# A conv, attention and expert kernel on one core: GpSimd's second addition of a round placed behind the first of the next

## The reference

```
x = x + conv3x3(groupnorm(x, 32 groups), sign(weight))
t = tokens(x)                                  # 3136 tokens of 64 channels per image
n = layernorm(t)
q, k, v = n Wq, n Wk, n Wv                     # one head of 32
t = t + softmax(q k^T / sqrt(32)) v Wo + b_o + n
n = layernorm(t)
w = softmax(mean over images of n, Wr)         # 8 gates per token
t = t + sum over 8 experts of w_e * (relu(bn(relu(bn(n W1_e)) W2_e)) Wo_e + bo_e)
```

## Time and profile before

| | |
|---|---|
| median of 3 runs | 7050.26 us (7049.38 to 7055.04) |
| the profiled execution | 7055.03 us, of which the span of instructions is 7053.2 |
| granted TensorE clock, mean | 0.986 |
| PE, POOL, DVE, ACT busy | 6827.4, 5472.6, 5077.8, 4355.5 us |
| a steady slot | 180.0 us |
| last attention slot (image 31) | about 5740 to 5902 us |
| start of the second block | about 5933 us |

### The profile page before, as it was taken

How to read it: one execution, slowest core, us unless ns; L and a number is a source line. 1 busy time by engine, 2 the same in 40 slices (tenths; PEclk the granted TensorE clock), 3 DMA queues, 4 the chain that set the end, 5 groups by cost and what they waited for, 6 DMA issues and landing times. The chain is left out here.

```text
span 7053.2 us, 132108 instructions
## 1 busy us (share of the span) xinstructions
PE 6827.4 (97%) x50610; PEld 3615.0 (51%) x50610; DVE 5077.8 (72%) x9184; ACT 4355.5 (62%) x9296; POOL 5472.6 (78%) x5522
## 2 busy tenths in 40 slices
PE   6999999999999999999999999999999997999999
PEld 3555555555555555555555555555555553333333
DVE  6777777777777777777777777777777762655565
ACT  1666666666666666666666666666666664555555
POOL 2888888888888888888888888888888895222222
PEclk7999999999999999999999999999999997999999
DMA  1111111111111111111111111111111002444443
GB/s 31 15 24 24 24 24 24 24 24 24 24 24 24 24 24 24 24 24 24 20 19 24 24 24 24 24 24 24 24 24 24 10 10 56 100 101 103 101 102 93
DMA packets 328980, 248.83 MB, mean 35 GB/s; under 512 B 253672, under 2 KB 311408, under 8 KB 324256
## 3 DMA queue, kind: packets, MB, share of 16 engines
q1 hardware_dynamic: 316064, 214.68, 13.7%
q0 software_dynamic: 12288, 25.71, 1.8%
HBM read 162.70 MB, written 77.59 MB: 34 GB/s over the span
## 5 line engine op out<-in xcount | busy, mean ns | idle before, releaser
L618 ACT ACTIVATE probs<-bank 128x392 f32<-128x392 f32 x6400 | 2796.9, 496 | 1887.0 <-PE bank L667 1841.0
L481 DVE TENSOR_REDUCE part_max<-bank 128x1 f32<-128x448 f32 x5600 | 3213.3, 614 | 583.9 <-PE bank L660 573.8
L660 PE MATMUL bank<-ks,qs 96*128 96x448 f32 x5600 | 2347.9, 424 | 55.3 <-DVE part_max L481 50.0
L428 POOL TENSOR_TENSOR psum<-psum,probs 128x392 f32<-128x392 f32 x2048 | 2098.6, 1025 | 318.3 <-ACT probs L618 33.1
L425 POOL TENSOR_TENSOR psum<-probs 128x392 f32<-128x392 f32 x2048 | 2099.5, 1025 | 240.9 <-ACT probs L618 229.5
L667 PE MATMUL bank<-qs,ks 97*128 97x392 f32 x6400 | 2027.4, 367 | 15.6 <-ACT probs L618 13.3
L676 PE MATMUL bank<-probs,vs 128*32 128x392 f32 x12288 | 1768.2, 507 | 34.1 <-POOL psum L428 26.6
L678 PE MATMUL bank<-psum,ones 128*32 128x392 f32 x4096 | 1740.7, 507 | 0.0
L660 PEld LDWEIGHTS bank<-ks,qs 96*128 96x128 f32 x5600 | 1065.5, 190 | 1230.8 <-DVE part_max L481 745.5
L667 PEld LDWEIGHTS bank<-qs,ks 97*128 97x128 f32 x6400 | 1191.7, 190 | 407.0 <-ACT probs L618 223.0
L985 ACT ACTIVATE h<-l_bank,xin 128x392 f32<-128x392 f32 x1024 | 639.0, 674 | 445.1 <-PE l_bank L1079 445.1
(11 more groups left out here) (126 smaller groups left out, 5740.3 us busy)
## 6 DMA issues: line engine op xcount, KB each, us to landing
xin<-in_x_dram SPq DMA_DIRECT2D x64, 784.0 KB, 8.9
xs<-x_dram SPq DMA_DIRECT2D x512, 98.0 KB, 2.5
xpk<-in_x_dram SPq DMA_DIRECT2D x64, 392.0 KB, 12.6
t_dram<-t SPq DMA_DIRECT2D x32, 784.0 KB, 5.3
x_dram<-xn SPq DMA_DIRECT2D x32, 784.0 KB, 6.9
res<-t_dram SPq DMA_DIRECT2D x256, 98.0 KB, 2.7
out_dram<-fin POOLq DMA_DIRECT2D x256, 98.0 KB, 2.8
gate_w<-gate_dram SPq DMA_DIRECT2D x16, 392.0 KB, 5.2
```

The source lines that it names most:

```text
L428: add = gp.tensor_tensor(into, into, three, ALU.add)
L481: v.tensor_reduce(part_max[:, b, m:m + 1], m_bank[place.bank()][:, 0:MW], AX.X, ALU.max).then_inc(m_used, 1)
L618: s.activation(probs[:, held(c, k), :], s_bank[n % 3][:, 0:2 * QW], ACT.Exp, scale=SCALE).then_inc(p_ready, 1)
L660: mm(m_bank[place.bank()][:, 0:MW], qs[par][0:KS, b * P:(b + 1) * P], ks[par][0:KS, m * MW:(m + 1) * MW], start=True, stop=True).then_inc( ...
```

## The change

In a round, the second add leaves the step `sum` and becomes a step of its own, `third`, whose place is 3.1 units (`GROUP + 0.1`) behind `sum`: just behind the `sum` of the next round, which is 3 units on. The add of the half block becomes the step `tail`, 2.8 units behind the last `third` of a chunk. Steps that fall past the slot's end go to `norms`. `sum_part` now counts first adds alone; a new semaphore `round_part` tells `tail` of the last `third`. What is added, and in which order within a round, is the same.

Beside it the places of other steps are changed: `sum` 0.29 units earlier, `apply` 1.2 later, `gather` 0.3 earlier; `stats` with 2.72 units between them instead of 2.18; `moments`, `pair` and `shift` (which hang on `PAD_AT`) 5.69 later, the four `pad` steps at 123.5, 140.4, 157.3 and 174.2 instead of 117.8, 135.5, 153.2 and 170.9; `conv` 1, `var` 1 and `var` 3 of `prepare` (with what hangs on them) by 0.4 to 0.7; `fetch` 0.37 and `store` 7.17 earlier. In the order that results, `moments` comes between the first and second reciprocal of the divide of c = 3 (before: ahead of `max` of block 7, 6), and `pair` between scores 20 and 21 of c = 4 on PE (before: between 14 and 15, ahead of `project` of c = 3).

```diff
--- before.py
+++ after.py
@@ -69,16 +69,16 @@
 DVE_LAG = 0
 VALUE_AFTER = HELD - VISIT
 VISIT_AT, DOOR = 0.0, 1
-SUM_LAG, APPLY_LAG = 1.22, 3.72
-GATHER_AFTER, DIVIDE_AFTER, DIVIDE_STEP = -0.19, 0.1, 0.73
-STATS_AT, STATS_STEP, PAD_AT, PAD_STEP = 93.6, 2.18, 117.81, 17.71
-PREPARE_AT = (0.4, 2.6, 5.3, 7.6, 19.2, 19.9, 25.4, 28.1, 30.6, 32.6, 35.9, 38.6)
+SUM_LAG, APPLY_LAG = 0.93, 4.92
+GATHER_AFTER, DIVIDE_AFTER, DIVIDE_STEP = -0.49, 0.1, 0.73
+STATS_AT, STATS_STEP, PAD_AT, PAD_STEP = 93.6, 2.72, 123.5, 16.9
+PREPARE_AT = (0.4, 2.6, 6.0, 7.6, 19.2, 19.9, 24.9, 28.1, 30.6, 32.6, 35.9, 39.0)
 NORMS_AT = (69.7, 74.5, 77.8, 81.9, 92.7, 95.9, 101.3, 106.5)
 PROJ_AT, PROJ_STEP = 12.23, 3.3
 VALUES_AT = (50.8, 58.0)
 BORDER, LAST_MAX = 58.0, 9.34
 ROW_AFTER = (1.2, 4.1)
-FETCH_AT, STORE_AT = 60.89, 113.0
+FETCH_AT, STORE_AT = 60.52, 105.83
 
 
 def visit_at(n):
@@ -116,7 +116,11 @@
         order += [(c * BLOCKS + k + 0.5, "attend", "score", (c, k)) for k in range(BLOCKS)]
         order.append((c * BLOCKS + BLOCKS - 0.3, "attend", "score", (c, BLOCKS)))
         for r in range(ROUNDS):
-            order.append((c * BLOCKS + GROUP * (r + 1) - 0.5 + SUM_LAG, "attend", "sum", (c, r)))
+            at = c * BLOCKS + GROUP * (r + 1) - 0.5 + SUM_LAG
+            order.append((at, "attend", "sum", (c, r)))
+            for kind, later in (("third", GROUP + 0.1), ("tail", GROUP - 0.2))[:1 + (r + 1 == ROUNDS)]:
+                at += later
+                order.append((at, "attend", kind, (c, r)) if at < SLOT else (at - SLOT, "norms", kind, (c, r)))
         for g in range(ROUNDS // TURN):
             at, stage = visit_at(c * ROUNDS // TURN + g)
             order.append((at, stage, "value", (c, g)))
@@ -307,7 +311,7 @@
         x_used = sem("x_used")
         conv_done, mean_done, sq_ready, var_done, rstd_ready, xn_ready, base_ready = (
             sem(n) for n in ("conv_done", "mean_done", "sq_ready", "var_done", "rstd_ready", "xn_ready", "base_ready"))
-        sum_part, sum_ready = sem("sum_part"), sem("sum_ready")
+        sum_part, round_part, sum_ready = sem("sum_part"), sem("round_part"), sem("sum_ready")
         m_done, part_hi, m_used = sem("m_done"), sem("part_hi"), sem("m_used")
         v_done = sem("v_done")
         rowmax_ready, row_bounced = sem("rowmax_ready"), sem("row_bounced")
@@ -416,23 +420,23 @@
                         inner = pad[C:P, 1 + rows.start:1 + rows.stop, 1:1 + HW]
                         gp.tensor_tensor(inner, xin[C:P, cols].rearrange("c (h w) -> c h w", w=HW), inner.bitcast(F32), ALU.subtract).then_inc(pad_lo, 1)
                         gp.wait_ge(pad_lo, im.count(CH, r + 1))
-                    elif kind == "sum":
+                    elif kind in ("sum", "third", "tail"):
                         c, r = a
                         first, rounds = c * KB + GROUP * r, c * ROUNDS + r
                         one, two, three = (probs[:, held(c, GROUP * r + n), :] for n in range(GROUP))
                         into = psum[:, rounds % SUMS, :]
-                        gp.wait_ge(p_ready, im.count(QC * KB, first + 2))
-                        gp.tensor_tensor(into, one, two, ALU.add).then_inc(sum_part, 1)
-                        gp.wait_ge(p_ready, im.count(QC * KB, first + 3))
-                        gp.wait_ge(sum_part, im.count(QC * (ROUNDS + 1), rounds + c + 1))
-                        add = gp.tensor_tensor(into, into, three, ALU.add)
-                        if r + 1 == ROUNDS:
-                            add.then_inc(sum_part, 1)
+                        if kind == "sum":
+                            gp.wait_ge(p_ready, im.count(QC * KB, first + 2))
+                            gp.tensor_tensor(into, one, two, ALU.add).then_inc(sum_part, 1)
+                        elif kind == "third":
+                            gp.wait_ge(p_ready, im.count(QC * KB, first + 3))
+                            gp.wait_ge(sum_part, im.count(QC * ROUNDS, rounds + 1))
+                            gp.tensor_tensor(into, into, three, ALU.add).then_inc(sum_ready if r + 1 < ROUNDS else round_part, 1)
+                        else:
+                            rest = slice(0, S - BLOCKS * P)
                             gp.wait_ge(p_ready, im.count(QC * KB, first + 4))
-                            gp.wait_ge(sum_part, im.count(QC * (ROUNDS + 1), rounds + c + 2))
-                            rest = slice(0, S - BLOCKS * P)
-                            add = gp.tensor_tensor(into[rest], into[rest], probs[rest, HELD, :], ALU.add)
-                        add.then_inc(sum_ready, 1)
+                            gp.wait_ge(round_part, im.count(QC, c + 1))
+                            gp.tensor_tensor(into[rest], into[rest], probs[rest, HELD, :], ALU.add).then_inc(sum_ready, 1)
                     elif (stage, kind) == ("prepare", "apply"):
                         q, = a
                         gp.wait_ge(rstd_ready, im.count(CH, q + 1))
```

## The result

The changed kernel takes **7039.32 us** (median of 9 runs, 7026.55 to 7053.02) beside 7055.74 for the kernel before (9 runs, 7049.38 to 7062.17): a ratio of 0.9977, interval 0.9967 to 0.9987. It is faster and inside the range, but by 16 us in the first measurement and 10 us in the second (7049.44 to 7039.34), where 31 us (0.44%) had been forecast.

A forecast was written before the change was run, and what follows sets the result against it. PE was taken to set the pace, with POOL late only at one wait a slot and the last slot's end. -11 - 14 - 6 = -31 us from 7050.3 gave 7019 us, 0.44% less; range 6992 to 7046.

The forecast's parts named there:

- The pause is a wait for the predecessor: POOL's third additions: start to start falls from 1.16 to 0.98 us, 0.18 us a round, 11.5 us of POOL a slot.
- rival three: POOL's adds: the pause is a cost of each instruction, so the change does nothing; about 7050 us, chance 0.03.
- Last slot: Image 31's attention slot, where POOL is the bound: 64 rounds save 0.18 us each; 11 us taken, between 8.6 and 12.
- Steady wait: PE's one wait a slot for POOL's `psum`, 0.47 us, goes whole in 30 slots: 14 us, bounds 0 and 16.
- The opening claim of the prediction: Steady slot of 180.0 us, PE busy 176.77: only 3.2 us of PE's own idle time can be won by removing waits.
- rival 4: The order also relieves DVE, 1 us a slot on top of POOL's gain: 6995 us, chance 0.10.
- Stage order: Moved steps around `project` of c = 3: -0.2 us a slot, -6 us in all, bounds +1.1 and -0.8 a slot.
- The stall ahead of pair: PE at the moved `pair` matmul waits for the divide: 1.55 us instead of 0.47 for `part_max`, +1.1 a slot, offset elsewhere.
- Rival 1: The moved pair costs more than POOL's wait gave: full stall 7071 us, or 7052 at +0.9 a slot; chances 0.06 and 0.10.
- Rival 2: Only the last slot gains, as PE's 0.47 us goes to ACT or DVE instead: 7039 us, chance 0.13.
- 7000 to 7036 by the bounds: Whole kernel: the span of times given to the forecast itself, chance 0.58.

The follow-up runs named there:

- split_only: The changed kernel with every place in the order as before, so only the step is split; 7016.3 us, ratio 0.9953 to the kernel before.
- back_both_one: `pair_back` with the shift and the second operation of moments in the form with one tensor input; 6976.8 us, ratio 0.9893 to the kernel before.
- pair_back: The changed kernel with stats, moments, pair and shift back at their places of before, pads as changed; 6998.5 us, ratio 0.9929.
- shift_one: The changed kernel with the shift taking one tensor input and a scalar for each partition; 7024.2 us, ratio 0.9961 to the kernel before.
- moments_back: `shift_one` with stats and moments back at their places of before, pair and shift still in the new place; 6994.4 us, ratio 0.9919.
- after_again: The changed kernel, unchanged, measured a second time; 7039.3 us, ratio 0.9985 to the kernel before.
- moments_early: The changed kernel with moments moved just ahead of the divide of chunk 3, pair still behind it; 7061.5 us, ratio 1.0020.
- pair_only: The kernel before, adds still chained, with only the places of stats, moments, pair, shift and pad as changed; 7078.2 us, ratio 1.0042.
- pair_118: `shift_one` with pair and shift 1.8 units later, moments still inside the divide; 7006.0 us, ratio 0.9930 to the kernel before.

## Why the prediction was right in sign and wrong in size

- **The pause is a wait for the predecessor, not a cost of each instruction: right.** 0.98 us a third add, idle time 0.0; rival three fell.
- **Last slot, -11 us: right.** 159.9 to 148.1 in the kernel after, 148.1 to 148.7 in every profiled kernel with the split, 159.8 to 160.0 in those without.
- **Steady wait, -14 us: right in mechanism, too small.** The wait for `psum` vanished in the kernels with the split (0.2 us once is left in two of them), and the slot of `split_only` is 0.80 us shorter, not 0.47. But this is not the 0.47 us won whole. Of the 10.3 us of the earlier trace rows, 6.8 came back as PE's wait for `part_max`, which rose from 32.4 to 39.2 us while `shift` had grown to 0.55; with both one-input forms (`back_both_one`) it is 32.1. The opening claim of the prediction, that only PE's idle time can be won, was wrong here. By the distances of starts over 22 slots, PE's idle time fell by only 0.16 us a slot in `split_only` (median, 3.21 to 3.05) and its other time by 0.65 (176.74 to 176.09), about half of it between `max` and score matmuls and the rest where one of these meets a value or pair matmul: delays too short to be booked as waits. Which engine's they were I didn't separate. For the same reason rival 4 was shut out too early by "the 32.4 us are what there is".
- **Stage order, -6 us: the step that failed.** On the split kernel the whole new order costs 23 us (7039.3 against 7016.3): the moved group +41 (against `pair_back`), the other places -18. On the kernel before, the line with stats and pads alone costs 29. Two things in it were wrong. (1) The working put the moved group into DVE's sum at its old duration, `shift` at 0.15 us. Its length depends on how it falls beside POOL's adds: 0.15 in the kernel before, 0.55 with the split alone, 0.85 with the move alone, and 2.39 with both, which is a 1.5 us delay of a slot. Without it the slot is 178.45 (`shift_one`), below the 179.2 that was forecast. The row that pointed to it was in the prediction: the second operation of moments, as small, at 0.88 us. (2) The stall ahead of pair was forecast at 1.55 us a slot with its time mostly given back, and that held: 1.10, and 0.07 us of slot time between `shift_one` and `moments_back`. What wasn't in the sum is what the clock does behind it and behind the wait that the long shift makes. 3.4 us at half clock cost 1.0 to 1.4 us, and it happened in 12 and 13 of 28 slots of the kernel after.
- **Rival 1** (the moved pair costs more than POOL's wait gave) named the place and not the price: it had the full stall as the cost. **Rival 2** gave 7039 us, the measured time, and outwardly this is what happened: only the last slot gained. In `split_only` DVE did take about two thirds of the booked wait, as this rival held; but that the steady slots gain nothing is refuted by its slot of 179.14 us and its 0.9953.
- **The range.** That 7039 lies inside it is two errors of opposite sign: the split gave 33 us instead of 25, and the new order cost 23 instead of giving 6. And "7000 to 7036 by the bounds" isn't what the prediction's bounds give: -12 - 16 - 24 makes 6998, and -8.6 - 0 + 33 makes 7075.
- The change would have had room for more than forecast: -33 from the split, -18 from the pads' and other places (`pair_back` against `split_only`), and some -8 and -14 from the two one-input forms.

Two things stay open: which end of a POOL instruction a waiting two-input operation gets, and why the clock falls behind a wait in one slot and not in the next. In three slots of `after_again` the shift took 0.44 us without a low clock (slots of 178.47), so the first may depend on how the two engines' instructions happen to lie, which I didn't control.

## What to carry to other kernels

Small VectorE operations beside a GpSimd stream are not small by their element count: look at their durations next to GpSimd's instructions, give them one tensor input where a scalar for each partition does, and look again once GpSimd's pauses are taken away. On a full TensorE, an idle time costs by what the granted clock does behind it as much as by its length: read the clock slot by slot, and keep what delays a bank's release out of the stretch where TensorE waits for it. And time a change of an operation apart from the change of order that comes with it; here the second hid more than half of the first.

## What the runs showed of the hardware

- A dependent GpSimd add starts 0.14 us behind the end of its predecessor (1.16 start to start), an independent one 0.04 us ahead of it (0.98). With one other instruction between, the dependent one pays nothing.
- A 128x1 VectorE operation with two SBUF tensor inputs took 0.15 us when it began in a pause of GpSimd (the kernel before). Begun inside a GpSimd instruction it ended about 0.02 us behind the end of one: at the first such end in all 29 slots of `split_only` (0.55 us) and `pair_back` (0.69), at the third in 20 of 28 slots of the kernel after (2.39). The longest, 4.69 us, was one of `moments_early`. With one tensor input and a scalar for each partition: 0.20 and 0.27 us.
- In otherwise full stretches of PE, 1.48 us of idle time ahead of one matmul were followed by half clock in 26 of 28 slots (`pair_only`), 1.1 in 9 to 15, 0.43 in none (`moments_back`); two waits of 0.3 and 0.6 us close together in 8 (`pair_118`). 11 stretches of 3.4 us cost 1.4 us each (`shift_one`).
- The first exp came at about 168 us in 8 of the 14 profiled executions and at about 173.5 in 6, whatever the order of steps, by when the granted clock first rose. No kernel was profiled in both groups.
